# Embedding gathers of 127 partitions on GpSimd, with the left-out rows copied one by one from SyncE

## The chip, the cores and the metric

One core of one Trainium2 chip runs the whole program. The time is device microseconds from start to end of one launch, as the median of a few runs. A profiled execution gives the trace.

## What is computed

A recommendation model (DLRM) over a batch of 2048 samples, all in float32. For each sample 26 table indices pick 26 rows of 64 floats, and a bottom network makes a 27th vector from 13 dense inputs:

```python
x = relu(dense @ Wb0 + bb0)            # 13 -> 512
x = relu(x @ Wb1 + bb1)                # -> 256
d = relu(x @ Wb2 + bb2)                # -> 64
sp = emb[arange(26)[None, :], sparse_idx]        # (2048, 26, 64) out of (26, 12500, 64)
T = concatenate([sp, d[:, None, :]], axis=1)     # (2048, 27, 64)
Z = einsum('bnd,bmd->bnm', T, T)                 # all dot products of a sample's 27 vectors
h = concatenate([d, Z[:, li, lj]], axis=1)       # 64 + 351
h = relu(h @ Wt0 + bt0)                # -> 512
h = relu(h @ Wt1 + bt1)                # -> 256
p = sigmoid(h @ Wt2 + bt2)             # -> 1
```

The rows of one sample lie at unrelated places of the tables, so 2048 x 26 = 53248 rows of 256 bytes have to be fetched by index.

## The kernel before

The batch is cut into 8 steps of 256 samples. A step's samples are two halves h of 128, one sample to a partition; `rows` holds, for each partition, 26 tables x 2 halves x 64 floats. One gather (line 260, `gather(t, h, landed)`) is an indirect DMA issued by GpSimd (POOL): it takes column 2t + h of `idx_step`, 128 indices, and brings 128 rows of 256 bytes into `rows[:, t, h*64:(h+1)*64]`. A step has 52 of them, the kernel 416. There is only one buffer of `rows`.

The 26 tables are grouped in 7 runs (`RUNS`): runs 0 to 5 have 4 tables, that is 8 gathers, run 6 has 2 tables, 4 gathers. Steps 0 to 6 are a loop on GpSimd (`pool.Fori(0, STEPS - 1)`); the last step is written out behind it, with half 0 of all tables ahead of half 1, so that its first half can be worked on early.

The order around the gathers is kept by semaphores:
- `begin(i, staged, hi)` on POOL waits until the index columns of the step are in `idx_step` (`head_staged` for runs 0 to 3, `rest_staged` for runs 4 to 6) and until the rows of the step before have been read out (`rows_turned`).
- PE's `turn(i, r)` (matmul at line 320) waits for all gathers of run r (`rows_landed[r]`), transposes its tables into PSUM and raises `rows_turned`, one count for each run. Line 334 is the same in the last step, `turn_last`.
- ScalarE (even runs, line 545) and VectorE (odd runs, line 683) copy the transposed rows to `vecs_st` and `vecs_mv`.
- PE's `gram(i, u)` (line 351) forms the dot products of 128 samples. VectorE transposes them (lines 693, 695), ScalarE packs them (line 568), PE transposes them back (line 383) and runs the top network (lines 394 to 431). The top network of step i - 1 stands between the `turn`s of step i.
- VectorE's `stage` (line 661) copies the next step's index columns from `idx_row` to `idx_step`, the head behind the copies of run 3, the rest behind the first transpose of the dot products. `idx_row`, the row numbers of all steps, clamped to their tables, is computed at the start in two pieces; `idx_done` reaches 8 when all of it is there (line 772).

SyncE (SP) issues the loads of indices and weights at lines 227 to 232, waits for `probs_ready` and stores the output (line 235). ScalarE issues seven more loads. The bottom network of four chunks of 512 samples runs before and during step 0 on PE, ScalarE and VectorE.

Of the kernel before, what the change touches and what calls it, by code (L numbers as in the profile page):

```python
# [35 lines left out]
P = 128  # L36
BATCH = 2048
TABLES = 26
VOCAB = 12500
DIM = 64  # L40
# [4 lines left out]
STEPS = BATCH // STEP  # L45
# [6 lines left out]
DSLOT = TABLES  # L52
# [12 lines left out]
RUNS = [(t, min(4, TABLES - t)) for t in range(0, TABLES, 4)]  # L65
NR = len(RUNS)
ACT_RUNS = (NR + 1) // 2
DVE_RUNS = NR // 2

HEAD = 4  # L70
HEAD_COLS = 2 * RUNS[HEAD][0]
STEP_COLS = 2 * TABLES
# [19 lines left out]
def build(nc, x, idx, emb, wb0, bb0, wb1, bb1, wb2, bb2, wt0, wt1, bt1, wt2, bt2, out):  # L92
    emb_rows = emb.rearrange("t v d -> (t v) d")

    with ExitStack() as ctx:  # L95
        def sb(name, shape, dt=F32):
            return ctx.enter_context(nc.sbuf_tensor(name, shape, dt))
# [4 lines left out]
        def sem(name):  # L102
            return ctx.enter_context(nc.semaphore(name))
# [20 lines left out]
        idx_row = sb("idx_row", [P, STEPS * STEP_COLS], I32)  # L124
        idx_step = sb("idx_step", [P, STEP_COLS], I32)
# [6 lines left out]
        rows = sb("rows", [P, TABLES, 2 * DIM])  # L132
# [24 lines left out]
        idx_done = sem("idx_done")  # L157
# [2 lines left out]
        gathers_begun = sem("gathers_begun")  # L160
        rows_landed = [sem(f"rows_landed{r}") for r in range(NR)]
        rows_landed_last = [[sem(f"rows_landed_last{h}_{r}") for r in range(NR)] for h in range(2)]
        rows_turned = sem("rows_turned")
        b0_summed = sem("b0_summed")
        b0_act = sem("b0_act")
# [59 lines left out]
        @block.sync  # L225
        def _(sp):
            sp.dma_start(idx_raw[:, :], idx).then_inc(idx_loaded, 16)
            sp.dma_start(wb0_sb[:, :], wb0).then_inc(bottom_loaded, 16)
            sp.dma_start(wb1_sb[:, :, :], wb1.rearrange("(k p) n -> p k n", p=P)).then_inc(bottom_loaded, 16)
            sp.dma_start(wb2_sb[:, :, :], wb2.rearrange("(k p) n -> p k n", p=P)).then_inc(bottom_loaded, 16)  # L230
            sp.dma_start(wt0_sb[:, :, :], wt0.rearrange("k p n -> p k n")).then_inc(top_loaded, 16)
            sp.dma_start(wt1_sb[:, :, :], wt1.rearrange("(k p) n -> p k n", p=P)).then_inc(top_loaded, 16)

            sp.wait_ge(probs_ready, 1)
            sp.dma_start(out.rearrange("(p n) -> p n", p=P), probs[:, :]).then_inc(out_stored, 16)
            sp.wait_ge(out_stored, 16)

        @block.gpsimd
        def _(pool):
            nc.gpsimd.iota(idx_base[:, :], [[0, STEPS], [VOCAB, TABLES], [0, 2]], base=0,  # L240
                           channel_multiplier=0).then_inc(base_ready, 1)

            pool.wait_ge(filled, 1)
            nc.gpsimd.affine_select(out=ident[:, :], in_=ones[:, :], pattern=[[-1, P]], compare_op=ALU.is_equal,
                                    fill=0.0, base=0, channel_multiplier=1).then_inc(ident_ready, 1)

            pool.sem_inc(rows_turned, NR)

            parts = ((head_staged, 0, HEAD // 2), (head_staged, HEAD // 2, HEAD), (rest_staged, HEAD, NR))

            def begin(i, staged, hi):

                pool.wait_ge(staged, i + 1)
                pool.wait_ge(rows_turned, i * NR + hi)

                pool.sem_inc(gathers_begun, 1)

            def gather(t, h, landed):
                c = 2 * t + h
                nc.gpsimd.indirect_dma_start(  # L260
                    rows[:, t, h * DIM:(h + 1) * DIM], None, emb_rows,
                    bass.IndirectOffsetOnAxis(idx_step[:, c:c + 1], 0)).then_inc(landed, 16)

            with pool.Fori(0, STEPS - 1) as i:
                for staged, lo, hi in parts:
                    begin(i, staged, hi)
                    for r in range(lo, hi):
                        first, n = RUNS[r]
                        for t in range(first, first + n):
                            for h in range(2):  # L270
                                gather(t, h, rows_landed[r])

            for h in range(2):
                for staged, lo, hi in parts:
                    if h == 0:
                        begin(STEPS - 1, staged, hi)
                    for r in range(lo, hi):
                        first, n = RUNS[r]
                        for t in range(first, first + n):
                            gather(t, h, rows_landed_last[h][r])  # L280

        @block.tensor
        def _(pe):
# [26 lines left out]
            def turn(i, r):  # L310

                first, n = RUNS[r]
                pe.wait_ge(rows_landed[r], (i + 1) * (32 * n))

                if r >= 2 and r % 2 == 0:
                    pe.wait_ge(vecs_act, i * ACT_RUNS + r // 2)
                if r >= 2 and r % 2 == 1:
                    pe.wait_ge(vecs_dve, i * DVE_RUNS + r // 2)
                for j in range(n):
                    turned = nc.tensor.transpose(ps_turn[r % 2][:, j, :], rows[:, first + j, :], ident[:, :])  # L320
                turned.then_inc(rows_turned, 1)

            def turn_last(h, r):
# [6 lines left out]
                if k >= 2 and k % 2 == 1:  # L330
                    pe.wait_ge(vecs_dve, (STEPS - 1) * DVE_RUNS + k // 2)
                cols = DIM * (h + 1)
# [4 lines left out]
            def gram(i, u):  # L337

                if u == 0:

                    pe.wait_ge(vecs_act, (i + 1) * ACT_RUNS)
                    pe.wait_ge(vecs_dve, (i + 1) * DVE_RUNS)
                    pe.wait_ge(d_placed, i + 1)
# [13 lines left out]
            def gram_last(h):  # L357
# [3 lines left out]
                pe.wait_ge(vecs_act, i * ACT_RUNS + (NR * (h + 1) + 1) // 2)  # L361
                pe.wait_ge(vecs_dve, i * DVE_RUNS + NR * (h + 1) // 2)
                if h == 0:
# [75 lines left out]
            def first_step():  # L439

                for c in range(FIRST_CHUNKS, CHUNKS):

                    pe.wait_ge(d_ready, c)
                    turn(0, 2 * (c - FIRST_CHUNKS))
                    turn(0, 2 * (c - FIRST_CHUNKS) + 1)
                    bottom_12(c, last=(c == CHUNKS - 1))

                pe.wait_ge(d_ready, CHUNKS)
                for r in range(2 * (CHUNKS - FIRST_CHUNKS), NR):
                    turn(0, r)  # L450
                gram(0, 0)
                gram(0, 1)
                turn_feat(0, 0)
                turn_feat(0, 1)
# [379 lines left out]
```

## Time and profile before

| | us |
|---|---|
| median of 2 runs | 551.62 (551.23 and 552.0) |
| span of the profiled execution | 551.0 |
| POOL busy | 394.4 (72%), 422 instructions |
| PE busy | 310.5 (56%) |
| ScalarE busy | 134.6 (24%) |
| VectorE busy | 127.8 (23%) |
| mean granted TensorE clock | 0.703 of 2.4 GHz |

Line numbers are those of the kernel before. "Busy" leaves out what an engine's sequencer does by itself, waits, register work and the issue of DMAs by SyncE and ScalarE. A releaser in brackets is what ended an engine's idle time; "issue" means that the profile shows nothing for which the engine waited. The end of a gather on POOL is the end of its issue, not the landing of its data.

### The profile page before, as it was taken

Reading aid. Unit: us, or ns where it says so; the run is one execution under the profiler, and the core shown is the slowest. Engines: PE = TensorE matmul, PEld = TensorE weight load, DVE = VectorE, ACT = ScalarE, POOL = GpSimd, SP = SyncE. Lnnn points to the kernel's source line nnn. Section 1 sums busy time; section 2 is a strip of 40 time slices with the busy share of each in tenths; the row PEclk is TensorE's granted clock in tenths of the full one; section 3 lists DMA queues with packets and bytes.
Section 4 is the critical chain, followed back from the end, with each engine's and each line's share of the span. In section 5 each row is a group of like instructions: output and inputs, shape, how many; then the busy total and the mean of one; then the engine's idle time right before and its main releaser. Section 6 shows DMA issues by size and latency. Waiting matters only on the chain.

```text
span 551.0 us, 8032 instructions
## 1 busy us (share of the span) xinstructions
PE 310.5 (56%) x3370; PEld 226.6 (41%) x3370; DVE 127.8 (23%) x190; ACT 134.6 (24%) x197; POOL 394.4 (72%) x422
## 2 busy tenths in 40 slices
PE   4799966825556327164373455552463742775566
PEld 1333325713445217152272334441253522664546
DVE  5213232222220222220212202302222112221110
ACT  1124333502242213122152021420133221311101
POOL 5777777777777777777777777777777777777710
PEclk9996796776586566675576765766667756795686
DMA  7233323333243322333233332343323432333310
GB/s 204 25 27 28 26 27 28 28 26 27 29 26 27 26 27 26 27 26 26 26 26 26 26 27 26 27 26 27 28 25 26 26 26 27 26 27 28 28 10 2
DMA packets 16181, 16.53 MB, mean 30 GB/s; under 512 B 7691, under 2 KB 8972, under 8 KB 16153
## 3 DMA queue, kind: packets, MB, share of 16 engines
q0 software_dynamic: 13312, 13.66, 31.7%
q1 hardware_dynamic: 2170, 2.41, 1.4%
q10 hardware_dynamic: 684, 0.24, 0.2%
q8 instruction: 12, 0.20, 0.1%
q14 instruction: 3, 0.02, 0.0%
HBM read 16.28 MB, written 0.01 MB: 30 GB/s over the span
## 4 chain that ended last, share of the span: by engine, by line
POOL 68%; issue 24%; PE 4%; DMA 2%; DVE 1%; POOLq 1%; ACT 1%; DVEq 0%; ACTq 0%
POOL rows L260 68%; DMA rows<-in_emb,idx_step 1%; PE ps_t L431 1%; DMA idx_raw<-in_idx 1%; PE ps_gram L351 1%; PE ps_t L400 1%; PE ps_gram L373 0%; PE ps_feat L400 0%; PE ps_turn L334 0%; ACT vecs_mv L545 0%; POOLq L95 0%; DVE gram_s L693 0%; DVE gram_s L695 0%; PE ps_feat L383 0%; PE ps_feat L394 0%
## 5 line engine op out<-in xcount | busy, mean ns | idle before, releaser
L260 POOL DMA_INDIRECT rows<-in_emb,idx_step x416 | 392.7, 944 | 130.8 <-issue 130.5
L320 PE MATMUL ps_turn<-ident,rows 128*128 128x128 f32 x182 | 41.0, 365 | 167.3 <-DMA rows<-in_emb,idx_step 162.1
L320 PEld LDWEIGHTS ps_turn<-ident,rows 128*128 128x128 f32 x182 | 26.2, 181 | 183.6 <-issue 174.3
L545 ACT ACTIVATE vecs_st<-ps_turn 128x512 f32<-128x512 f32 (+1 forms) x28 | 25.9, 926 | 215.2 <-PE ps_turn L320 215.0
L351 PE MATMUL ps_gram<-vecs_mv,vecs_st 128*32 128x54 f32 x1792 | 43.5, 296 | 25.2 <-ACT vecs_mv L545 13.3
L545 ACT ACTIVATE vecs_mv<-ps_turn 64x512 f32<-64x512 f32 (+1 forms) x56 | 54.0, 964 | 0.3
L351 PEld LDWEIGHTS ps_gram<-vecs_mv,vecs_st 128*32 128x32 f32 x1792 | 40.8, 173 | 29.3 <-issue 13.8
L431 PE MATMUL ps_t<-wt_sb,ht_t 128*128 128x256 f32 x128 | 52.0, 578 | 0.0
L683 DVE COPY vecs_st<-ps_turn 128x512 f32<-128x512 f32 x21 | 21.3, 1014 | 120.5 <-PE ps_turn L320 120.5
L683 DVE COPY vecs_mv<-ps_turn 64x512 f32<-64x512 f32 x42 | 43.7, 1042 | 0.3
L431 PEld LDWEIGHTS ps_t<-wt_sb,ht_t 128*128 128x128 f32 x128 | 36.4, 298 | 15.4 <-issue 8.2
L706 DVE SCALAR_TENSOR_TENSOR ht_w<-ps_t,wt_sb 128x256 f32<-128x256 f32 x16 | 6.8, 424 | 136.6 <-PE ps_t L431 136.6
L693 DVE STREAM_TRANSPOSE gram_s<-ps_gram 128x864 f32<-128x864 f32 x16 | 17.3, 1083 | 82.1 <-PE ps_gram L351 67.7
L400 PE MATMUL ps_t<-feat_t,wt_sb 117*128 117x128 f32 x192 | 34.3, 328 | 0.6 <-ACT feat_t L574 0.6
L297 PE MATMUL ps_t<-hb,wb_sb 128*128 128x512 f32 x64 | 31.7, 653 | 3.3 <-DVE hb L668 3.3
L400 PEld LDWEIGHTS ps_t<-feat_t,wt_sb 117*128 117x128 f32 x192 | 31.2, 240 | 0.9 <-ACT feat_t L574 0.9
L400 PE MATMUL ps_feat<-feat_t,wt_sb 117*128 117x128 f32 x192 | 29.7, 296 | 0.0
L400 PEld LDWEIGHTS ps_feat<-feat_t,wt_sb 117*128 117x128 f32 x192 | 27.4, 215 | 0.0
L568 ACT ACTIVATE feat<-gram_s 128x351 f32<-128x351 f32 x16 | 13.4, 840 | 56.0 <-DVE gram_s L695 56.0
L297 PEld LDWEIGHTS ps_t<-hb,wb_sb 128*128 128x128 f32 x64 | 13.4, 216 | 21.1 <-issue 16.3
L383 PE MATMUL ps_feat<-ident,feat 128*117 128x128 f32 x48 | 12.5, 383 | 14.5 <-ACT feat L568 14.5
L421 PE MATMUL ps_t<-bt_sb,ones 1*128 1x256 f32 x32 | 17.3, 637 | 0.0
(52 smaller groups left out, 235.8 us busy)
## 6 DMA issues: line engine op xcount, KB each, us to landing
rows<-in_emb,idx_step POOLq DMA_INDIRECT x416, 3.4
wt_sb<-in_wt SPq DMA_DIRECT2D x1, 1024.0 KB
wb_sb<-in_wb SPq DMA_DIRECT2D x1, 512.0 KB
wt_sb<-in_wt SPq DMA_DIRECT2D x1, 512.0 KB
idx_raw<-in_idx SPq DMA_DIRECT2D x1, 208.0 KB, 3.9
wt_sb<-in_wt ACTq DMA_DIRECT2D x1, 128.0 KB
x_t<-in_x ACTq DMA_DIRECT2D x1, 104.0 KB
wb_sb<-in_wb SPq DMA_DIRECT2D x1, 64.0 KB
```

The costliest lines, as they stand in the source:

```text
L260: nc.gpsimd.indirect_dma_start(rows[:, t, h * DIM:(h + 1) * DIM], None, emb_rows, bass.IndirectOffsetOnAxis(idx_step[:, c:c + 1], 0)).then ...
L297: summed = nc.tensor.matmul((ps_t0, ps_t1)[m][:, :], wb1_sb[:, k, m * P:(m + 1) * P], hb0[:, k, :], start=(k == 0), stop=(k == B0 // P - 1))
L320: turned = nc.tensor.transpose(ps_turn[r % 2][:, j, :], rows[:, first + j, :], ident[:, :])
L351: summed = nc.tensor.matmul(ps_gram[32 * v:32 * v + 32, b, g * 2 * VECS:(g + 1) * 2 * VECS], vecs_st[:, c, :], vecs_mv[:, c, :, :].rearran ...
L383: turned = nc.tensor.transpose(ps_feat[u][0:PAIR_ROWS, k, :], feat[:, u, k * PAIR_ROWS:(k + 1) * PAIR_ROWS], ident[:, :])
L400: summed = nc.tensor.matmul(top_0_blocks(u, m // 2)[:, m % 2, :], wt0_sb[0:PAIR_ROWS, k, m * P:(m + 1) * P], feat_t[:, u, k, :], start=Fal ...
L421: nc.tensor.matmul(ps_t1[:, 0:T1], ones[0:1, :], bt1_sb[:, :], start=True, stop=False)
L431: summed = nc.tensor.matmul(ps_t1[:, 0:T1], ht0_t[:, k, :], wt1_sb[:, k, :], start=False, stop=(k == T0 // P - 1))
L545: moved = nc.scalar.activation(to, source, ACT.Copy)
L568: nc.scalar.activation(feat[:, u, :].rearrange("p (e i) -> p e i", e=DELTAS), bass.AP(gram_s[u], SLOTS, [[WRAP * SLOTS, P], [SLOTS, DELTAS ...
L683: moved = nc.vector.tensor_copy(to, source)
L693: nc.vector.transpose(gram_s[u][:, 0:VECS * SLOTS], unit_products(VECS)).then_inc(gram_turned, 1)
```

## The change

The looped steps gather `rows[0:n]` in place of `rows[:]`: n is 127 in all runs but run 5, and there 128, 128, 126, 124, 120, 112, 127 and 127 for its eight gathers (`MIXED_ROWS`). The rows of the partitions n to 127 are fetched by SyncE. In a loop over the same steps and runs it waits for `rows_turned` of the run in the step before, loads the row numbers of one partition from `idx_row` into registers (`load_rows`), and issues one DMA of one row for each of them, with the row number from the register (`fetch`). The DMAs of a run raise `left_landed[r]`, and PE's `turn` waits for it too. The last step is not changed. The gathers of table 25 also differ in a flag (`oob_is_err`), which for the others is as it would be by default. The whole diff:

```diff
--- before.py
+++ after.py
@@ -66,6 +66,22 @@
 NR = len(RUNS)
 ACT_RUNS = (NR + 1) // 2
 DVE_RUNS = NR // 2
+
+
+MIXED = 5
+MIXED_ROWS = (P, P, P - 2, P - 4, P - 8, P - 16, P - 1, P - 1)
+
+
+def gathered(t, h):
+    r, first = t // 4, 4 * (t // 4)
+    return MIXED_ROWS[2 * (t - first) + h] if r == MIXED else P - 1
+
+
+def left_rows(r):
+    first, n = RUNS[r]
+    return sum(P - gathered(t, h) for t in range(first, first + n) for h in range(2))
+
+
 
 HEAD = 4
 HEAD_COLS = 2 * RUNS[HEAD][0]
@@ -160,6 +176,7 @@
         gathers_begun = sem("gathers_begun")
         rows_landed = [sem(f"rows_landed{r}") for r in range(NR)]
         rows_landed_last = [[sem(f"rows_landed_last{h}_{r}") for r in range(NR)] for h in range(2)]
+        left_landed = [sem(f"left_landed{r}") for r in range(NR)]
         rows_turned = sem("rows_turned")
         b0_summed = sem("b0_summed")
         b0_act = sem("b0_act")
@@ -231,6 +248,28 @@
             sp.dma_start(wt0_sb[:, :, :], wt0.rearrange("k p n -> p k n")).then_inc(top_loaded, 16)
             sp.dma_start(wt1_sb[:, :, :], wt1.rearrange("(k p) n -> p k n", p=P)).then_inc(top_loaded, 16)
 
+            def fetch(t, h, p, row, r):
+                sp.dma_start(rows[p:p + 1, t, h * DIM:(h + 1) * DIM],
+                             emb_rows[bass.ds(row, 1), :]).then_inc(left_landed[r], 16)
+
+            def load_rows(i, p, lo, hi):
+                _, values = nc.values_load_multi_w_load_instructions(
+                    idx_row[p:p + 1, bass.ds(i * STEP_COLS + lo, hi - lo)], engines=(mybir.EngineType.SP,),
+                    min_val=0, max_val=TABLES * VOCAB - 1,
+                    skip_runtime_bounds_check_because="the indices were clamped to their tables on the chip")
+                return values
+
+            sp.wait_ge(idx_done, 8)
+            with sp.Fori(0, STEPS - 1) as i:
+                for r in range(NR):
+                    first, n = RUNS[r]
+                    sp.wait_ge(rows_turned, i * NR + (r + 1))
+                    for p in range(P - 1, min(gathered(t, h) for t in range(first, first + n) for h in range(2)) - 1, -1):
+                        cols = [2 * t + h for t in range(first, first + n) for h in range(2) if gathered(t, h) <= p]
+                        values = load_rows(i, p, cols[0], cols[-1] + 1)
+                        for c in cols:
+                            fetch(c // 2, c % 2, p, values[c - cols[0]], r)
+
             sp.wait_ge(probs_ready, 1)
             sp.dma_start(out.rearrange("(p n) -> p n", p=P), probs[:, :]).then_inc(out_stored, 16)
             sp.wait_ge(out_stored, 16)
@@ -255,11 +294,12 @@
 
                 pool.sem_inc(gathers_begun, 1)
 
-            def gather(t, h, landed):
+            def gather(t, h, landed, n=P):
                 c = 2 * t + h
                 nc.gpsimd.indirect_dma_start(
-                    rows[:, t, h * DIM:(h + 1) * DIM], None, emb_rows,
-                    bass.IndirectOffsetOnAxis(idx_step[:, c:c + 1], 0)).then_inc(landed, 16)
+                    rows[0:n, t, h * DIM:(h + 1) * DIM], None, emb_rows,
+                    bass.IndirectOffsetOnAxis(idx_step[0:n, c:c + 1], 0),
+                    oob_is_err=(t != DSLOT - 1)).then_inc(landed, 16)
 
             with pool.Fori(0, STEPS - 1) as i:
                 for staged, lo, hi in parts:
@@ -268,7 +308,7 @@
                         first, n = RUNS[r]
                         for t in range(first, first + n):
                             for h in range(2):
-                                gather(t, h, rows_landed[r])
+                                gather(t, h, rows_landed[r], gathered(t, h))
 
             for h in range(2):
                 for staged, lo, hi in parts:
@@ -311,6 +351,7 @@
 
                 first, n = RUNS[r]
                 pe.wait_ge(rows_landed[r], (i + 1) * (32 * n))
+                pe.wait_ge(left_landed[r], (i + 1) * (16 * left_rows(r)))
 
                 if r >= 2 and r % 2 == 0:
                     pe.wait_ge(vecs_act, i * ACT_RUNS + r // 2)
```

## Rows read from the trace of the kernel before

**Rows 1.** The page: chain that ended last, shares of the span by engine and line.

```profile
POOL 68%; issue 24%; PE 4%; DMA 2%; DVE 1%; POOLq 1%; ACT 1%; DVEq 0%; ACTq 0%
POOL rows L260 68%; DMA rows<-in_emb,idx_step 1%; PE ps_t L431 1%; DMA idx_raw<-in_idx 1%; PE ps_gram L351 1%; PE ps_t L400 1%; PE ps_gram L373 0%; PE ps_feat L400 0%; PE ps_turn L334 0%; ACT vecs_mv L545 0%; POOLq L95 0%; DVE gram_s L693 0%; DVE gram_s L695 0%; PE ps_feat L383 0%; PE ps_feat L394 0%
```

**Rows 2.** Groups of instructions, POOL: count | busy us, mean ns | idle before, releaser.

```profile
L260 POOL DMA_INDIRECT rows<-in_emb,idx_step x416 | 392.7, 944 | 130.8 <-issue 130.5 <-DVE idx_step L661 0.3
```

**Rows 3.** Time windows, POOL alone: window, length, busy (instructions), clock, DMA share, GB/s.

```profile
84.00:148.90 64.90, 49.06 (x52) 0.66 0.34 28
148.90:213.80 64.90, 49.06 (x52) 0.66 0.35 27
```

**Rows 4.** Timeline of POOL, its last two gathers: start, duration, instruction [idle before].

```profile
523.68 0.94 POOL L260 DMA_INDIRECT rows<-in_emb,idx_step  x1 [0.30 <-issue]
524.93 0.95 POOL L260 DMA_INDIRECT rows<-in_emb,idx_step  x1 [0.30 <-issue]
```

**Rows 5.** Waits: waiting engine <- releaser: us in total, times, longest.

```profile
ACT vecs_st L545 <- PE ps_turn L320: 215.0, 23, 14.1
...
PE ps_turn L320 <- DMA rows<-in_emb,idx_step: 162.1, 35, 9.8
...
SPq L235 <- ACT probs L653: 545.4, 1, 545.4
```

**Rows 6.** The page: DMA queues, packets, MB, share of 16 engines.

```profile
q0 software_dynamic: 13312, 13.66, 31.7%
q1 hardware_dynamic: 2170, 2.41, 1.4%
```

**Rows 7.** Issues of DMAs: KB each, median us from issue to landing; gathers, output.

```profile
rows<-in_emb,idx_step POOLq DMA_INDIRECT x416, 3.4
...
out<-probs SPq DMA_DIRECT2D x1, 8.0 KB, 1.4
```

**Rows 8.** Timeline: indices ready, staging for the step that begins at 266.51.

```profile
7.10 0.54 DVE L772 CUSTOM_DVE_ANT_0 idx_row<-idx_raw,idx_base 128x728 uint16<-128x728 uint16 x1
...
247.61 0.18 DVE L661 COPY idx_step<-idx_row 128x32 int32 x1
...
266.51 0.94 POOL L260 DMA_INDIRECT rows<-in_emb,idx_step  x1 [0.30 <-issue]
...
269.02 0.69 PE L320 MATMUL ps_turn<-ident,rows 128*128 128x128 f32 x2 [4.13 <-DMA rows<-in_emb,idx_step]
...
276.31 0.13 DVE L661 COPY idx_step<-idx_row 128x20 int32 x1
```

**Rows 9.** Timeline of the DMA issues of SyncE, and small ones of ScalarE.

```profile
0.81 0.39 SPq L227 DMA_DIRECT2D idx_raw<-in_idx  x1
1.26 0.44 SPq L228 DMA_DIRECT2D wb_sb<-in_wb  x1
...
3.25 0.51 SPq L232 DMA_DIRECT2D wt_sb<-in_wt  x1
549.21 0.37 SPq L235 DMA_DIRECT2D out<-probs  x1
...
1.48 0.37 ACTq L628 DMA_DIRECT2D bb_sb<-in_bb  x1
1.89 0.44 ACTq L629 DMA_DIRECT2D bb_sb<-in_bb  x1
2.36 0.52 ACTq L630 DMA_DIRECT2D bb_sb<-in_bb  x1
```

**Rows 10.** Timeline: an instruction of VectorE that reads a value back.

```profile
240.08 0.08 DVE L706 DVE_READ_ACCUMULATOR ht_w<-ps_t,wt_sb  x1
```

## The prediction

> **What bounds the kernel now.** I read the chain of work that ended last first [rows 1]. The reader sees one engine in it: GpSimd (POOL) with 68% of the span, all at line 260, the indirect gather, and 24% "issue". The groups of instructions for POOL [rows 2] say what that issue time is: 416 gathers of 944 ns each, and 130.5 us of idle time before them that nothing in the profile releases, about 0.3 us a gather. The time windows [rows 3] hold 52 gathers in 64.9 us, in two steps one behind the other, so the pitch is 64.9 / 52 = 1.248 us, of which 0.94 is busy. The timeline at the end [rows 4] shows the last gather starting at 524.93. So the kernel is a row of 416 gathers at a fixed pitch, and then a tail of 551.0 - 524.93 = 26.1 us in which TensorE, VectorE and ScalarE finish the last half step. The list of waits [rows 5] agrees: PE spends 162.1 us waiting for gathers to land, ScalarE 215.0 us waiting for PE. SyncE (SP) waits 545.4 us in one piece for the probabilities: it issues six loads at the start and then has nothing to do.
>
> Two prices follow. One nanosecond off each gather's pitch in the seven loop steps is worth 7 x 52 = 364 ns. One microsecond of work of another engine per step is worth nothing while its step fits in 64.9 us, and 7 us as soon as it does not.
>
> **What the change takes from POOL.** In each of the seven looped steps 50 of the 52 gathers lose rows: 46 of them one row, one each 2, 4, 8 and 16. That is 76 rows of 52 x 128 = 6656, 1.1%. The last step (52 gathers, no loop) stays as it is. No row of the trace shows a gather of another size. From below: if the whole pitch went by rows, 1.248 x 76 / 128 = 0.74 us a step, 5.2 us in all. If nothing of it does, 0. A gain beyond that is possible only if 127 rows are worked on in another way than 128, and the trace has a hint of how large such a piece could be: the software queue moved 13312 packets [rows 6], 32 for each of 416 gathers. These are 16 of data and 16 small ones, one of each per DMA engine. 0.944 us / 32 is 30 ns a packet; if 127 rows were written as 8 data packets of 16 rows on one engine instead of 16, that is 8 x 30 = 0.24 us less, 0.24 x 322 gathers of 127 rows = 77 us. On the other side, if the rows of 16 engines are now written side by side and would have to be written one after another, a gather could cost several times 0.94 us. I take half the proportional value, 0 to 5 us, as "unchanged", because the gathers differ by only 1 row in 128 and the row they are nearest to is that of 128; both ends stay in the range.
>
> The Trainium skill (DMA: Bandwidth & Descriptors, section Why a DMA increments its semaphore by 16 and not by 1) says that a transfer runs on the largest number of engines up to 16 that divides its slowest dimension, so that 127 partitions go on one engine, though some direct copies from GpSimd are exempt. The trace before has only 128, which shows both kinds of packet on all sixteen. By that rule the landing of a gather changes, and possibly its generation.
>
> What a longer landing would do can be had from rows: the software queue fills 31.7% of 16 engines' span [rows 6], 0.317 x 16 x 551 / 416 = 6.7 us of engine time a gather. On one engine that would be in series, and landing goes from 3.4 us [rows 7] to about 3.4 + 6.7 x 15/16 = 9.7 us. POOL would not feel it: the index columns that its next step needs are staged at 247.61 and 276.31, and it uses them at 266.51 and, 32 gathers later, at 306.4 [rows 8]. There are 18 and 30 us of slack against 6.3 us.
>
> **What the change gives to SyncE.** Per looped step and run of tables: one wait on the transposes of the step before, then register loads of the indices of one partition, then one DMA of 256 bytes for each row left out. Runs 0 to 4 have one register load and 8 DMAs each, run 6 one load and 4 DMAs. Run 5 has 16 loads (partitions 127 down to 112) and 32 DMAs. Sum: 22 loads and 76 DMAs a step, 154 and 532 in all.
> - DMA issue: the six loads that SyncE issues back to back start at 0.81 and end at 3.76 [rows 9], 2.95 / 6 = 0.49 us each with the gap. Smaller transfers are hardly cheaper: ScalarE's small ones took 0.37 to 0.52, and the 8 KB output 0.37. So 76 x 0.49 = 37.2 us a step; by 0.37 it would be 28.1.
> - Register loads: none in this trace. From below, the cheapest instruction that brings a value back is a 0.08 us read of VectorE's accumulator [rows 10]: 22 x 0.08 = 1.8 us. From above, a small DMA and its receipt: the output took 1.4 us from issue to landing [rows 7]: 22 x 1.4 = 31 us; if each of the 76 values needed its own load, 106 us. A load sends a request to SBUF and must have the answer before the DMA behind it can go, so it is nearest to that round trip without its issue, 1.4 - 0.37 = 1.03 us: 22 x 1.03 = 22.7 us.
> - Address arithmetic: a multiplication and an addition per row. The nearest row is the gap between two DMAs on the queue, 0.06 us (1.20 to 1.26) [rows 9]: 76 x 2 x 0.06 = 9.1 us; from below 0, if the DMA takes the register as it is.
>
> Sum for SyncE: 37.2 + 22.7 + 9.1 = 69.0 us a step, against POOL's 64.9. Its bounds are 28.1 + 1.8 = 30 us and 37.2 + 106 + 9.1 = 152 us.
>
> The Trainium skill (DMA: Bandwidth & Descriptors, section Latency and other measured facts) gives a floor of about 600 ns for a load of registers. With it the loads would be 22 x 0.6 = 13.2 us and SyncE's step an estimated 59.5 us, below POOL's; with one load per value it would be 91.9 us. No row here shows either.
>
> **How a long SyncE step reaches the end.** SyncE may run a full step ahead: its DMAs for run r of step i + 1 wait only for the transposes of run r of step i. So the burst in run 5 is spread over a step, and only the sum per step counts. If that sum is above POOL's, transpose(i, r) on PE waits for SyncE. Behind it wait the copies of ScalarE and VectorE, then VectorE's staging of the next indices, then POOL, whose slack is used up within a few steps. The end is then: indices ready at 7.6 [rows 8], seven SyncE steps, 1.4 landing, 7.4 from the transposes of run 6 to the staged indices (269.02 to 276.44) [rows 8], then 36 gathers of the last step, of which the last starts 35 x 1.248 = 43.7 later, and the tail of 26.1. With S for SyncE's step that is 86.2 + 7 S. It equals 551 at S = 66.4. At 69.0 it is 569.2.
>
> The extra wait of PE before each run costs only when it has to wait. The 532 rows are 0.14 MB beside 13.66, nothing for the DMA engines.
>
> **Forecast:** 569.2 in the profiled span. The span before is 551.0 and the median of its runs 551.62, so 570 us.
>
> **The rivals.**
> - SyncE stays hidden (S below 66.4) and POOL's gathers cost what they did: 551.6 less 0 to 5, 549. For it: a register load at 0.6 or address arithmetic for nothing is enough. Against it: it needs a sum below 66.4 from 98 items of which 76 already take 37.2. This is also the case in which the change does not do what it says for POOL.
> - Faster: a gather of 127 rows is a cheaper kind of instruction and SyncE is short enough. With 0.24 us less on 322 gathers the end of POOL's chain is at 551 - 77 = 474; it decides at S = (474 - 86.2) / 7 = 55.4, above that SyncE gives the time: 506 at S = 60, and no gain from 66.4 on. For it: the packet count; against it: nothing else in the trace says that one row matters.
> - Slower through POOL: 127 rows are dearer. 0.1 us more on 322 gathers gives 551.6 + 32 = 584; twice the pitch, 1.25 us more, gives 954. For it: rows that are now spread evenly, 8 to an engine, no longer can be. The deciding point is 0.034 us a gather, 11 us in all. By the skill's rule on 127 partitions this or the rival above is what happens.
>
> **How the numbers follow.** SyncE as the bound with POOL's gathers near their old price: 0.40 (0.04 of it between 551 and 563). Hidden and unchanged: 0.22. Cheaper gathers and a short SyncE: 0.22, of it 0.01 less than 2%. Dearer gathers: 0.16. What this kernel's measurement tells from no change is about 2%, 11 us: slower 0.36 + 0.16 = 0.52, same 0.22 + 0.04 + 0.01 = 0.27, faster 0.21. The range 480 to 690 leaves out 0.08 below (gathers much cheaper and S under 56) and 0.12 above (S over 86, as with a load per value, or gathers at over 1.4 times their price). The likeliest case alone would be 552 to 690.
>
> **What the profile of the changed kernel would show.** If I am right, the list of waits has PE's transposes waiting for row DMAs of SyncE instead of gathers, the chain consists of SyncE's queue, POOL has gaps at the step boundaries, and a step takes 69 us. A register load that takes well under 0.8 us makes the forecast wrong at once, since each 0.1 us there is 2.2 us a step and 15 us in the end. The gathers' own durations, 940 ns or not at 127 rows against the two of 128 in run 5, decide between the last two rivals whatever SyncE does. A landing near 10 us instead of 3.4 would show the single engine.

## The result and the profile after

The changed kernel takes 1202.96 us (median of 2 runs, 1202.16 to 1203.76) against 551.62 before: 2.183 times as long, 95% interval 2.179 to 2.187. The span of its profiled execution is 1200.4 us. Its page, first the busy times of the engines (us, share of the span, instructions), then the chain that ended last, then the software queue of GpSimd's gathers and SyncE's queue (packets, MB, share of 16 engines):

```profile
PE 326.9 (27%) x3370; PEld 238.0 (20%) x3370; DVE 134.8 (11%) x190; ACT 134.6 (11%) x197; POOL 914.9 (76%) x422
...
POOL 75%; issue 22%; PE 1%; DMA 1%; POOLq 0%; DVE 0%; ACT 0%; ACTq 0%; DVEq 0%
...
q0 software_dynamic: 49488, 15.99, 28.5%
q1 hardware_dynamic: 3234, 2.55, 0.7%
```

POOL is the chain now as it was in [rows 1]. There is no SyncE in it. The group of the gathers, which answers to [rows 2]:

```profile
L299 POOL DMA_INDIRECT rows<-in_emb,idx_step x416 | 913.3, 2195 | 260.9 <-issue 260.9
```

The same 416 gathers are busy for 520.6 us more (913.3 - 392.7), and POOL's idle time before them is 130.1 us more (260.9 - 130.8). Together that is 650.7, and the tail behind the last gather is 1.3 us shorter: the whole of the 649.4 us between the two spans. The timeline of POOL around run 5 of the fourth step shows both, and which gathers they belong to:

```profile
604.44 2.54 POOL L299 DMA_INDIRECT rows<-in_emb,idx_step  x1 [0.31 <-issue]
611.24 2.55 POOL L299 DMA_INDIRECT rows<-in_emb,idx_step  x1 [4.26 <-issue]
614.09 0.96 POOL L299 DMA_INDIRECT rows<-in_emb,idx_step  x1 [0.30 <-issue]
615.35 0.95 POOL L299 DMA_INDIRECT rows<-in_emb,idx_step  x1 [0.30 <-issue]
616.61 0.99 POOL L299 DMA_INDIRECT rows<-in_emb,idx_step  x1 [0.30 <-issue]
617.91 1.32 POOL L299 DMA_INDIRECT rows<-in_emb,idx_step  x1 [0.30 <-issue]
619.53 0.98 POOL L299 DMA_INDIRECT rows<-in_emb,idx_step  x1 [0.30 <-issue]
620.82 0.95 POOL L299 DMA_INDIRECT rows<-in_emb,idx_step  x1 [0.30 <-issue]
622.08 2.55 POOL L299 DMA_INDIRECT rows<-in_emb,idx_step  x1 [0.30 <-issue]
624.93 2.55 POOL L299 DMA_INDIRECT rows<-in_emb,idx_step  x1 [0.30 <-issue]
```

From 614.09 on stand the gathers of 128, 128, 126, 124, 120, 112, 127 and 127 rows. 127 rows take 2.55 us and 128 take 0.95. The price does not follow the number of rows: 126, 120 and 112 take 0.95 to 0.99, 124 takes 1.32. And there is a pause of 4.26 us before the last gather of run 4. There are 35 such pauses of 3.7 to 4.6 us (an ordinary gap is 0.30), five in each looped step, before the eighth gather of runs 0 to 4. None stands in run 5 or 6. The two gathers of table 25, which have the other flag, take 2.55 us like the rest.

SyncE's own queue, by line: kind of instruction, count, duration in ns (min/median/max), first and last start. A row costs it a register operation, a move and a DMA issue:

```profile
L252 SPq FUSED_REGOPS  x532: 37/37/37, 8.7 to 981.1; - x178
L252 SPq MOVE rows<-in_emb x532: 29/29/38, 8.8 to 981.2; - x178
L252 SPq DMA_DIRECT2D rows<-in_emb x532: 224/225/775, 8.8 to 981.3; - x178
...
L256 SPq TENSOR_LOAD <-idx_row x154: 438/776/2437, 7.9 to 979.4; - x154
```

and what SyncE waited for, which answers to the last line of [rows 5] (us in total, times, longest):

```profile
SPq L256 <- PE ps_turn L361: 568.4, 33, 44.4
SPq L274 <- ACT probs L694: 216.9, 1, 216.9
```

It waits for PE for 568 us in all, so it is ahead of PE and not behind it. The run without its copies, below, takes the same time.

### The profile page after: what moved, and what is told of

Read it like the earlier page. It is cut to its first block, busy times and chain, and to the rows that moved or that the text cites. A ratio compares the mean times of both kernels' runs of the same rounds, so it can differ in the third digit from the quotient of the medians.

```text
span 1200.4 us, 10049 instructions
## 1 busy us (share of the span) xinstructions
PE 326.9 (27%) x3370; PEld 238.0 (20%) x3370; DVE 134.8 (11%) x190; ACT 134.6 (11%) x197; POOL 914.9 (76%) x422
## 3 DMA queue, kind: packets, MB, share of 16 engines
q1 hardware_dynamic: 3234, 2.55, 0.7%
## 4 chain that ended last, share of the span: by engine, by line
POOL 75%; issue 22%; PE 1%; DMA 1%; POOLq 0%; DVE 0%; ACT 0%; ACTq 0%; DVEq 0%
POOL rows L299 75%; DMA rows<-in_emb,idx_step 1%; DMA idx_raw<-in_idx 0%; PE ps_gram L414 0%; PE ps_t L441 0%; PE ps_feat L441 0%; PE ps_t L472 0%; POOLq L111 0%; PE ps_turn L361 0%; DVE gram_s L734 0%; PE ps_feat L424 0%; PE ps_feat L435 0%; ACT feat L609 0%; POOLq L293 0%; DVE gram_s L736 0%
## 5 line engine op out<-in xcount | busy, mean ns | idle before, releaser
L299 POOL DMA_INDIRECT rows<-in_emb,idx_step x416 | 913.3, 2195 | 260.9 <-issue 260.9
L361 PE MATMUL ps_turn<-ident,rows 128*128 128x128 f32 x182 | 50.3, 427 | 762.2 <-DMA rows<-in_emb,idx_step 750.5
L361 PEld LDWEIGHTS ps_turn<-ident,rows 128*128 128x128 f32 x182 | 31.5, 212 | 782.2 <-issue 537.1
L392 PE MATMUL ps_gram<-vecs_mv,vecs_st 128*32 128x54 f32 x1792 | 39.2, 272 | 25.3 <-ACT vecs_mv L586 13.3
L392 PEld LDWEIGHTS ps_gram<-vecs_mv,vecs_st 128*32 128x32 f32 x1792 | 36.4, 155 | 29.8 <-issue 13.8
L441 PE MATMUL ps_t<-feat_t,wt_sb 117*128 117x128 f32 x192 | 39.6, 365 | 0.6 <-ACT feat_t L615 0.6
L441 PEld LDWEIGHTS ps_t<-feat_t,wt_sb 117*128 117x128 f32 x192 | 37.3, 282 | 0.9 <-ACT feat_t L615 0.9
L346 PE MATMUL ps_turn<-hb,wb_sb 128*64 128x512 f32 x16 | 10.9, 819 | 40.9 <-DVE hb L715 40.9
L435 PE MATMUL ps_t<-d_t,wt_sb 65*128 65x128 f32 x64 | 18.4, 385 | 0.0
```

The costliest lines, as they stand in the source:

```text
L299: nc.gpsimd.indirect_dma_start(rows[0:n, t, h * DIM:(h + 1) * DIM], None, emb_rows, bass.IndirectOffsetOnAxis(idx_step[0:n, c:c + 1], 0), ...
L392: summed = nc.tensor.matmul(ps_gram[32 * v:32 * v + 32, b, g * 2 * VECS:(g + 1) * 2 * VECS], vecs_st[:, c, :], vecs_mv[:, c, :, :].rearran ...
L435: nc.tensor.matmul(top_0_blocks(u, m // 2)[:, m % 2, :], wt0_sb[0:D_ROWS, PAIR_TILES, m * P:(m + 1) * P], d_t[:, u, :], start=True, stop=F ...
L441: summed = nc.tensor.matmul(top_0_blocks(u, m // 2)[:, m % 2, :], wt0_sb[0:PAIR_ROWS, k, m * P:(m + 1) * P], feat_t[:, u, k, :], start=Fal ...
```

## The experiments

Two theories stood against each other at first. By the first all of the loss is in gathers that cannot be spread over 16 engines. By the second, that of the forecast, SyncE's new queue has a part in it. The second group of runs asks what the price of a gather goes by, the third what the pauses are, and the last whether SyncE's queue can be put to use. The runs that leave rows at zero (all but the first and the last two) were timed once each; their readings rest on the durations in their traces.

**SyncE's half alone.** The gathers are whole; the 76 copies a step go to a tile of their own.

```diff
-                                gather(t, h, rows_landed[r], gathered(t, h))
+                                gather(t, h, rows_landed[r])
-                sp.dma_start(rows[p:p + 1, t, h * DIM:(h + 1) * DIM],
+                sp.dma_start(spare[p:p + 1, t, h * DIM:(h + 1) * DIM],
```

> Only SyncE's half of the change: all gathers have 128 rows as before, and SyncE makes the same 76 row copies a step, into a tile of their own that nobody reads; PE still waits for them. Theory (all of the loss is in the gathers of 127, SyncE's step of about 59 us is hidden behind POOL's 64.9): 551 to 554 us. Rival, the one forecast before (SyncE's queue is longer than POOL's step): 562 us or more, with PE's transposes waiting for SyncE's copies. A second rival (the copies slow the gathers or the other engines by their traffic): a gather longer than 0.944 us.

Measured: 551.32 us (10 runs), ratio 1.000 with the interval 0.9986 to 1.0014. The gathers take 944 ns at the median as before. SyncE's copies, its loads, and its waits:

```profile
L253 SPq DMA_DIRECT2D spare<-in_emb x532: 224/225/311, 8.9 to 423.2; - x178
...
L257 SPq TENSOR_LOAD <-idx_row x154: 438/662/1520, 7.9 to 421.2; - x154
...
SPq L275 <- ACT probs L695: 124.4, 1, 124.4
SPq L257 <- PE ps_turn L362: 64.3, 14, 6.2
```

SyncE's loop runs from 7.9 to 423.4 and waits 64.3 us of that for PE: (423.4 - 7.9 - 64.3) / 7 = 50.2 us of work a step, under POOL's 64.9. It costs nothing that the runs can tell. The forecast's mechanism, a SyncE step longer than POOL's, is refuted.

**POOL's half alone.** The same sizes of gathers, no copies; the rows left out stay zero from one clearing at the start.

```diff
+            nc.vector.memset(rows[:, :, :], 0.0).then_inc(rows_cleared, 1)
-                    rows[:, t, h * DIM:(h + 1) * DIM], None, emb_rows,
-                    bass.IndirectOffsetOnAxis(idx_step[:, c:c + 1], 0)).then_inc(landed, 16)
+                    rows[0:n, t, h * DIM:(h + 1) * DIM], None, emb_rows,
+                    bass.IndirectOffsetOnAxis(idx_step[0:n, c:c + 1], 0)).then_inc(landed, 16)
```

> Only POOL's half of the change: gathers of 127 (run 5: 128, 128, 126, 124, 120, 112, 127, 127), the left-out rows stay zero (cleared once at the start), no copies by SyncE. Theory: 1200 us, gathers of 127 at 2.55 us and the same pauses of about 4 us before every eighth gather of runs 0 to 4. Rival (the copies add to it, for instance by making the pauses): about 1200 - 35 x 3.9 = 1065 us.

Measured: 1200.2 us, POOL 913.2 us busy, 260.9 us idle, 35 pauses at the same places. The two halves add up: within 3 us all of the loss is POOL's, and the pauses do not come from SyncE.

**Which sizes cost what.** All gathers whole but those of run 5.

```diff
+MIXED_ROWS = (122, 61, 124, 31, 113, 64, 16, 13)
```

> All gathers have 128 rows but the eight of run 5, which have 122, 61, 124, 31, 113, 64, 16 and 13; the other rows stay zero. Theory (a gather's busy time is about 0.84 us + 0.0134 us for each row on its fullest engine, the rows being spread over the largest number of engines up to 16 that divides their count): 1.66, 1.66, 1.26 to 1.31 twice, 2.36, 0.89, 0.85, 0.85 us, in all about 575 us. Rival (the price goes by the number of rows in all once they are not spread over 14 or more engines): 61 costs half of what 122 does above the fixed part, and 31 a quarter of 124. Second rival (an awkward size, whatever it is, costs 1.6 us): 61, 31 and 113 all at 2.5 us.

Measured: 575.6 us. "Engines" are the 16 DMA engines, over which the rows of a gather are divided. The durations of the eight gathers, read one by one off POOL's timeline in the third step, beside the division that the theory supposes:

```
rows   engines  rows on the fullest   busy us   0.84 + 0.0134 x that
122       2            61               1.68          1.66
61        1            61               1.68          1.66
124       4            31               1.29          1.26
31        1            31               1.27          1.26
113       1           113               2.37          2.35
64       16             4               0.91          0.89
16       16             1               0.86          0.85
13       13             1               0.88          0.85
```

The pairs decide it: 122 and 61 rows cost the same, and 124 and 31. It is neither the number of rows nor the odd size, but how many rows fall on the fullest of the engines, if they are spread over the largest number of engines up to 16 that divides their count. 127 rows give 0.84 + 127 x 0.0134 = 2.54, as measured. The formula is good to some hundredths of a us; the furthest off are the 124 rows of the changed kernel, 1.32 for 1.26.

The Trainium skill (DMA: Bandwidth & Descriptors, section Why a DMA increments its semaphore by 16 and not by 1) states this division, and with it that 127 partitions go on one engine. The runs agree for gathers: eight sizes fall on one line by it.

**Half the rows.** All 52 gathers of a looped step have 64 rows; the rest stays zero.

```diff
+def gathered(t, h):
+    return 64
```

> All 52 gathers of the looped steps have 64 rows (16 engines, 4 rows each), half of what 128 have; the rows of the other partitions stay zero, no copies by SyncE. Theory (0.84 us and 0.0134 us for each row on the fullest engine): 0.89 to 0.92 us busy, pitch 1.21, 551 - 364 x 0.04 = 536 us. Rival (the price goes by rows, so that leaving rows out pays if their number divides by 16): 0.5 us busy, 551 - 364 x 0.45 = 387 us.

Measured: 536.6 us. The gathers at 0.90, which were at 0.94 with 128 rows [rows 4]:

```profile
200.01 0.90 POOL L266 DMA_INDIRECT rows<-in_emb,idx_step  x1 [0.30 <-issue]
201.22 0.91 POOL L266 DMA_INDIRECT rows<-in_emb,idx_step  x1 [0.30 <-issue]
```

So even without an awkward number, leaving out half of the rows would be worth 15 us, and SyncE would have to fetch 64 x 52 rows a step for it, which at 0.41 us each is 1364 us.

**The pauses.** Now 127 rows in run 5 as well, no copies.

```diff
+def gathered(t, h):
+    return P - 1
```

> All 52 gathers of the looped steps have 127 rows, run 5 too, no copies by SyncE. It is made to tell what sets the pauses of about 4 us. Rival (it hangs on the run, as eight gathers that raise the same semaphore): a pause before the eighth gather of runs 0 to 5, none in run 6, at the same places in each step: 42 pauses, 1295 us.

Measured: 1291.5 us with 42 pauses, before gathers 7, 15, 23, 31, 39 and 47 of every step, counted from 0. One of them, and the landing of the gather that starts at 248.53:

```profile
248.53 2.55 POOL L266 DMA_INDIRECT rows<-in_emb,idx_step  x1 [0.30 <-issue]
254.95 2.55 POOL L266 DMA_INDIRECT rows<-in_emb,idx_step  x1 [3.88 <-issue]
...
DMA to landing us min/median/max: 5.8/5.8/5.8
```

The ring, as it was stated (every 8 gathers straight on), fails: between gather 47 of a step and 7 of the next stand 12 gathers and no pause. The next three runs try what could restart the count.

```diff
-            with pool.Fori(0, STEPS - 1) as i:
+            for i in range(STEPS - 1):
```

> As the run with 127 rows in all gathers, but GpSimd's loop over the seven steps is written out, so that no branch stands between steps. In that run the pauses stood before gathers 7, 15, 23, 31, 39 and 47 of each step, with only 11 gathers between the last of one step and the first of the next. Theory (the place of the pause is counted from the loop's branch): now every 8 gathers through, at 55, 63, ..., 45 of them: about 1302 us. Rival (it hangs on the runs, or on the semaphore that the eight gathers of a run share): the same places as before, 1291 us.

Measured: 1290.2 us, the pauses at the same places. The loop's branch is not it.

```diff
-                        for t in range(first, first + n):
-                            for h in range(2):
+                        for t in range(first + n - 1, first - 1, -1):
+                            for h in (1, 0):
```

> As the run with 127 rows in all gathers, but each run's gathers are issued in the reverse order, the last column of indices first. Theory (a pause is set by how many gathers have gone before in the run): still before the eighth gather of each of runs 0 to 5. Rival (it is set by the address of the index column or of the destination, the eighth of a run): before the first gather of each run, six a step. The time is near 1291 us in both.

Measured: 1292.0 us, again before the eighth gather issued, though that is now the first column of the run. Addresses are not it either.

```diff
-                                gather(t, h, rows_landed[r], gathered(t, h))
+                                gather(t, h, (rows_landed, rows_landed_b)[h][r], gathered(t, h))
```

> As the run with 127 rows in all gathers, but the eight gathers of a run raise two semaphores, four each, in turn. Theory (the pause of about 4 us comes with the eighth gather on one semaphore): no pause within a run, 1291 - 42 x 3.6 = 1140 us. Rival (the semaphore has nothing to do with it): 42 pauses at the same places, 1291 us.

Measured: 1174.8 us. Neither expectation holds: the 42 pauses are where they were, but POOL's idle time falls from 287.0 to 169.9 us, 117.1 / 42 = 2.8 us a pause, which is one pitch of a gather. One of them, and the landing of the gather that starts at 222.85:

```profile
222.85 2.55 POOL L267 DMA_INDIRECT rows<-in_emb,idx_step  x1 [0.30 <-issue]
225.71 2.55 POOL L267 DMA_INDIRECT rows<-in_emb,idx_step  x1 [0.30 <-issue]
229.33 2.55 POOL L267 DMA_INDIRECT rows<-in_emb,idx_step  x1 [1.08 <-issue]
...
DMA to landing us min/median/max: 5.9/5.9/5.9
```

What a pause waits for can be read from these traces, though the profile calls its idle time "issue". In the run with 127 rows and one semaphore, the gather behind each of the 42 pauses starts 0.60 us after the gather before the pause has landed (0.599 to 0.605, while the landing itself takes 5.7 to 6.7 us). The 35 pauses of the changed kernel do the same. With two semaphores it starts 0.58 us after the last gather but one has landed, the latest on its own semaphore; the gather between is still under way. So a pause is a wait of POOL for a landing, and two semaphores make it a landing one gather earlier.

Two sizes more, each on one engine, ask whether the pause needs many descriptors or merely slow gathers:

```diff
+def gathered(t, h):
+    return 61      # the other run: 113
```

> All 52 gathers of the looped steps have 61 rows, on one engine; the others stay zero, no copies. Without pauses: 1.68 us busy, pitch 1.98, 551 + 364 x 0.73 = 817 us. Made to size the pauses. 
Measured: 814.9 us, 1.67 us busy, and no pause at all.

> All 52 gathers of the looped steps have 113 rows, a prime, so again one engine and nearly the generation time of 127 (2.36 us, pitch 2.67); the rest stays zero, no copies. Rival (any run of eight slow gathers has it, 61 rows were merely not slow enough, for they land before the next is issued): 42 pauses of 3 to 3.6 us, 1190 to 1220 us.

Measured: 1219.2 us, 42 pauses, so the time is the rival's. But they stand before gathers 8, 16, 24, 32, 40 and 48 of each step, one later than with 127 rows. Gather 8 is the first of run 1, on another semaphore than gathers 0 to 7:

```profile
235.67 2.36 POOL L266 DMA_INDIRECT rows<-in_emb,idx_step  x1 [0.30 <-issue]
241.87 2.36 POOL L266 DMA_INDIRECT rows<-in_emb,idx_step  x1 [3.85 <-issue]
```

Here too the gather behind each pause starts 0.62 us after the one before it has landed, the last gather of the run before.

What has gone before the first pause of a step is 7 gathers of 127 rows or 8 of 113. With a descriptor more for each semaphore, the next would bring it to 8 x 128 = 1024 and 9 x 114 = 1026 for one engine. That speaks for a count of descriptors near 1024 and against the run and the eighth gather as such. It is argued and not shown, and three things do not fit it. The count would have to start anew with each step. From one pause to the next stand eight gathers with 127 rows too, 1024 descriptors, where at the start of a step seven are the most. And 61 rows show no pause with 52 x 62 descriptors. So what a pause waits for and what it costs is shown; why it comes at these gathers stays open.

**SyncE doing a whole gather.** If SyncE has room, it can take something whole. From the second step on it does table 25, half 1: 128 rows from its own copy of the indices in one partition, 8 to a register load, then one copy into `rows`. GpSimd has 51 gathers left. All of the reference is computed.

```diff
+            with sp.Fori(1, STEPS) as i:
+                for k in range(0, P, LOAD):
+                    ... LOAD = 8 registers from line_row[0:1, bass.ds(i * P + (k - P), LOAD)]
+                        sp.dma_start(last_st[k + j:k + j + 1, bass.ds(i - 1, 1), :].rearrange("p s d -> p (s d)"),
+                                     emb_rows[bass.ds(values[j], 1), :]).then_inc(copies_landed, 16)
+                sp.wait_ge(copies_landed, i * (16 * P))
+                sp.wait_ge(rows_turned, i * NR + NR)
+                sp.dma_start(rows[:, DSLOT - 1, DIM:2 * DIM], ...).then_inc(copies_placed, 16)
```

> What SyncE's idle queue can give: from the second step on it does one whole gather of each step (table 25, half 1) as 128 single rows, with indices from one partition, 8 to a register load, into a tile of its own with a place for each step, and one copy of that tile into the rows. GpSimd has 51 gathers in these steps, all of 128 rows. By the other runs SyncE needs 128 x 0.41 + 16 x 0.88 + 2.5 = 69 us a step and starts with a lead of a step, so it is in time for all seven: 551.6 - 7 x 1.248 = 543 us, ratio 0.984. Rival (SyncE falls behind, since 69 us is more than the 63.7 of GpSimd): PE waits for its copy in the last steps and the time is 551 or more.

Measured: 816.1 us, ratio 1.482 (1.479 to 1.484). The issue of a row took SyncE 529 ns in place of 225:

```profile
L257 SPq DMA_DIRECT2D last_st<-in_emb x896: 528/529/1207, 11.4 to 788.3; - x180
```

In the trace's operands each of these DMAs has 16 pieces of 16 bytes, those of the changed kernel one piece of 256. From one to the next it is 0.74 us, and SyncE's step is 111 us. In one more run the tile has a single place at a fixed address, and SyncE waits until the tile of the step before has been copied out:

```diff
-        last_st = sb("last_st", [P, STEPS - 1, DIM])
+        last_st = sb("last_st", [P, DIM])
+                sp.wait_ge(copies_placed, i * 16)
...
-                        sp.dma_start(last_st[k + j:k + j + 1, bass.ds(i - 1, 1), :].rearrange("p s d -> p (s d)"),
+                        sp.dma_start(last_st[k + j:k + j + 1, :],
```

> As the run in which SyncE does one whole gather a step, but the tile for its rows has one place at a fixed address instead of one for each step. There each row copy was cut into 16 pieces of 16 bytes and took 0.53 us to issue, 0.74 us from one to the next, so that SyncE's step was 111 us; here each is one piece of 256 bytes, as in the changed kernel. Theory (what a copy costs SyncE is its number of pieces): 0.23 us and 0.41 us, SyncE's step 71 us, in time for all seven gathers: 543 us, ratio 0.984. Rival (the issue is slow because two addresses stand in registers or because 896 follow each other): above 600 us again.

Measured: 544.2 us, ratio 0.987 (0.985 to 0.989) to the kernel before: faster than both kernels, if by only 1.3%.

```profile
L259 SPq DMA_DIRECT2D last_st<-in_emb x896: 224/225/315, 12.0 to 516.1; - x180
...
SPq L263 <- PE ps_turn L360: 7.8, 1, 7.8
...
L292 POOL DMA_INDIRECT rows<-in_emb,idx_step x409 | 386.2, 944 | 128.7 <-issue 124.1
```

Seven gathers fewer at 1.248 us are 8.7 us; 7.3 were measured. SyncE's step is 72 us, longer than POOL's 63.7, and it waits only once for PE: it lives on the lead of one step. Its last copy into `rows` is issued at 517.7 and POOL's last gather at 516.3, so there is no room for an eighth gather.

The edit takes two things away at once, the 16 pieces and the register in the destination's address. The copy of the tile into `rows` has 128 pieces in both runs, and there only the register goes (first the run at 816 us):

```profile
L261 SPq DMA_DIRECT2D rows<-last_st x7: 567/568/581, 120.1 to 790.2; - x7
...
L263 SPq DMA_DIRECT2D rows<-last_st x7: 508/514/551, 87.3 to 517.7; - x7
```

By that an address from a register is an estimated 0.05 us of the 0.30 between 529 and 225 ns, and the cut into pieces the rest; no run has the one without the other.

## Why the prediction was wrong

- **What bounds the kernel**: right. The row of gathers at a fixed pitch sets the end before and after, and the tail is 24.8 us after the last gather's start, 26.1 before. The price derived from it, 364 ns for each ns of pitch, holds: (2.55 - 0.94) x 322 gathers = 518 us of the 520.6.
- **What the change takes from POOL**: this is the step that failed. It gave 127 rows the price of 128, "because the gathers differ by only 1 row in 128". The price goes by the rows on the fullest engine, 8 with 128 rows and 127 with 127. The prediction had the mechanism as its lower-ranked side, rows written one after another instead of side by side, and from the Trainium skill the rule that 127 partitions go on one engine, and still gave it 0.16. It priced it at up to twice the pitch, 954 us, where the pitch is 2.855 / 1.248 = 2.29 times and pauses come on top. Its other use of the packet count was wrong in sign: a gather of 127 rows has more packets, not fewer. In the run with only those it is (54080 - 52 x 32) / 364 = 144 of them against 32 [rows 6]. The packet sizes in its trace give, for each gather, 7 of 4096 bytes and one of 3840, which are 127 rows; 105 of 64 bytes and 15 of 60, which are 15 times 127 entries of 4 bytes; and 16 of 4 bytes. The bytes fit: (16.34 MB - 1.71) / 364 = 40.2 KB a gather, that is 32.5 of rows and 7.6 of small entries. So the fifteen other engines seem to be filled up to the length of the fullest; the trace does not say which engine a packet is on.
- **The pauses**: 130 us that no part of the prediction had. They are waits of POOL for a landing.
- **Landing**: forecast to be 9.7 us, found 5.9 in the run with 127 rows only. The single engine was right, though the landing near 10 us that was to show it did not come; the term of 6.7 us of engine time was not right: the 16 data packets of 8 rows take 6.6 us in all in the trace before, the 8 packets of a gather of 127 rows only 2.0. What the landing gained besides is the writing of the entries, 2.55 us for 0.94; the first data packet starts 3.4 us after its gather does. The prediction gave POOL slack of 18 and 30 us against a later landing, and POOL indeed never waits for the indices. But it does wait for a landing in each pause: 5.9 - 2.55 + 0.60 = 3.95 us. So the landing on one engine has a part in the 130 us, by a wait that the prediction did not have.
- **SyncE's queue**, the likeliest case at 0.40: wrong; in this half the rival in which SyncE stays hidden (0.22) was right. Its sum was 69.0 us a step and is 50.2 in the run with the copies alone. A row is 0.41 us from one to the next where 0.49 + 0.12 were taken: the DMA issue itself is 0.225 us, less than the 0.37 of the smallest one in [rows 9], and the two register operations are 0.066. A load of registers is 0.66 us where 1.03 was chosen between bounds. By these, 76 x 0.41 + 22 x (0.66 + 0.16) = 49. The floor of about 600 ns for a load, which the prediction set beside the sum from the Trainium skill (DMA: Bandwidth & Descriptors, section Latency and other measured facts), gave 59.5 and would have put SyncE below POOL. The trace goes below that floor: the loads of one value took 0.44.
- **How a long SyncE step reaches the end**: not tried by this change. The run at 816 us had such a step, 111 us, in another kernel, and follows a formula of that kind: 11 us to SyncE's first copy, 7 x 111 = 777, and 24 from its last to the end are 812, near the span of its profile (812.6). The prediction's own constant, 86.2, was not tried.
- **The range** stopped at 690. It took "several times 0.94 us" as a bound and then weighted it at "over 1.4 times" with less than 0.12.

The sentence on what would decide held to the letter: the durations of the gathers of 127 rows beside those of 128 in run 5 settle the case.

## What to carry to other kernels

Before the count of partitions of a gather is changed, divide it: what counts is the rows on the fullest engine when they are spread over the largest divisor up to 16, and every row there costs GpSimd 13.4 ns on top of 0.84 us and a gap of 0.3. So 128 rows are nearly as cheap as 16, a prime number above 16 is the worst choice, and the saving that counts is a gather fewer. An idle SyncE can take one, at 0.41 us a row and 0.1 us for its index, if every copy is one piece with a fixed destination.

When a cost is not in the trace and a rule says that it changes its kind at this very size, the nearest row is not near: the two prices belong on both sides of the forecast with like weight.

## What the hardware showed that was not expected

- A gather's busy time against the rows on its fullest engine: 0.86 us at 1, 0.90 at 4, 0.944 at 8, 1.27 at 31, 1.68 at 61, 2.37 at 113, 2.55 at 127. Half the rows on 16 engines save 0.04 us.
- POOL pauses, for 3.5 to 4.9 us in all runs with one semaphore, after 7 gathers of 127 rows or 8 of 113, never with 61. A pause ends 0.60 us after the gather before it has landed (0.62 with 113 rows). It shrinks by 2.8 us when neighbouring gathers raise different semaphores.
- A DMA issue of SyncE with its source row in a register takes 225 ns as one piece and 529 ns as 16 pieces of 16 bytes with a second register in its address, though the same 256 bytes move. The large loads of [rows 9] are between at 0.39 to 0.51.
- A register load by SyncE takes 0.44 us for one value, 0.66 for two, 0.87 for three and 1.51 for six, but 0.72 for eight (medians of the run with the copies alone; 0.52 and 0.69 for the eights of the last two runs). Beside the gathers of 127 rows the 154 loads take 140 us in all, beside those of 128 rows 102.
